# Setup of a graph and expert kernel: edges in 96 and 15 rows, weights loaded behind x and worked on behind table 1

## The chip, the cores and the metric

The kernel runs on one core of a Trainium2 chip. Its engines are TensorE (PE), VectorE (DVE), ScalarE (ACT), GpSimd (POOL) and SyncE (SP); sixteen DMA engines move data for all of them. The metric is the device time of one execution in microseconds, here the median of three runs.

## The reference

Four layers act on x, 6250 nodes by 256 features, each added to x. With LN the layer norm of a row:

```
h   = LN(x)
x  += GRU(segment_sum(h[src] + relvectors[edge_type], dst), h)      # 100000 edges, sorted by dst
x  += shared_mlp(LN(x)) + sum over the top 2 of 4 experts           # small experts
x  += segment_sum((LN(x) @ W.T + b)[src_i], tgt_i) / (deg + 1)
x  += top 2 of 8 experts, 256 -> 1024 -> 256 with gelu, on LN(x)
```

## The kernel before

The program is a sequence of blocks. In each, every engine has its own list of instructions, which it works through in order; semaphores order them among each other, and between two blocks all engines meet at a barrier. The first block is the setup. Behind it come the gather of layer 0 (POOL fetches rows of a table in DRAM, 128 edges an instruction, L748; PE adds them up by products with one-hot matrices, L817), the second gather, the experts, and the combination at the end.

The setup does three things.

The **edges**: SP waits until DVE has filled three tiles `edge_i` and then loads `dst`, `src` and `edge_type_16`. Each array has 100000 numbers, laid out as 896 to a partition: 111 full rows (L342) and a row of 544 (L344). The semaphore `edges_loaded` rises by 16 with each DMA. DVE turns them to floats (L485) and computes from them, in a long chain of small instructions (L489 to L587), which edges each tile of 128 nodes needs; PE turns them (L664), and DVE copies the turned ones (L514).

**x and table 1**: SP, behind the edges, issues x as one DMA (L347: 128 partitions, 48 rows of 1 KB each) and its tail of 106 rows (L349); they signal `x_loaded` and `x_tail_loaded`. `table1_groups` then runs over 12 groups of four tiles, two at a time in two sets of buffers, and a last group of one tile. For each group DVE takes the row statistics (`variance`, L193 and L197), ACT the square root (`ln_sqrt`, L214), DVE the reciprocal (L202), the two copies for later (L639, L640) and the normalised rows `h` (L207), ACT their half-precision copy `part` (L440), DVE the rest that the copy leaves (L648), and SP stores both as 512 KB of `table1` (L359), waiting for each store to land before the next.

The **weights**: ACT issues 30 loads (L403), 3.3 MB in all, many of them small or in 4-byte pieces, once the edges have landed. When the last of them has landed, ACT copies three of them to a reduced precision (L447 to L449), PE transposes the GRU's matrices and the second graph layer's into six banks (L698), ACT takes the high part of each (L457), DVE the low part (L614), and the last matrix only scaled (L619). DVE's `raw_copied` tells PE when a bank is free again.

Before the change the weights' part stands ahead of `table1_groups` in the lists of ACT and DVE, so the order on both is: weights, then table 1. The order of everything is written by hand; no scheduler has a part in it. `setup_chain` is a semaphore by which DVE waits for its own earlier results.

Of the kernel before, what the change touches and what calls it, by code (L numbers as in the profile page):

```python
# [16 lines left out]
F32 = mybir.dt.float32  # L17
# [3 lines left out]
ALU = mybir.AluOpType  # L21
# [4 lines left out]
P = 128  # L26
N = 6250
D = 256
C = D // P
# [9 lines left out]
EP, EJ = 112, 7  # L39
# [12 lines left out]
SCALE = 2048.0  # L52
# [13 lines left out]
TURN_CREDIT = 3  # L66
# [4 lines left out]
def program(nc, a, out):  # L71
# [6 lines left out]
    with ExitStack() as ctx:  # L78
        def sem(name):
            return ctx.enter_context(nc.semaphore(name))  # L80

        def sb(name, shape, dt, where=None):
            return (where or ctx).enter_context(nc.sbuf_tensor(name, shape, dt))

        bank = [ctx.enter_context(nc.psum_tensor(f"bank{i}", [P, 512], F32)) for i in range(8)]
# [46 lines left out]
        consts_ready = sem("consts_ready")  # L132
        loads_done = sem("loads_done")
        x_loaded = sem("x_loaded")
        x_tail_loaded = sem("x_tail_loaded")
# [83 lines left out]
        weights = {}  # L219

        Wr = sb("Wr", [P, C, E1], F32, graph)
        gcnT = sb("gcnT", [P, C, D], F32, graph)
# [19 lines left out]
        def split_wt(name, shape):  # L242
# [3 lines left out]
        wihT = split_wt("wihT", [P, C, 3 * D])  # L246
        whhT = split_wt("whhT", [P, C, 3 * D])
# [5 lines left out]
        sW3 = split_wt("sW3", [P, 1, D])  # L253
        eW2 = wt("eW2", [P, E0, 64])
        eW3 = split_wt("eW3", [P, 2, D])
        sel = sb("sel", [G_ROWS, E0 * 64], FR, layer0)
        bih = wt("bih", [P, 6])
        bhh = wt("bhh", [P, 6])
        brz = wt("brz", [P, 4])
        b_l1 = wt("b_l1", [P, 6])  # L260
        b_l2 = wt("b_l2", [P, 3])
        b_l3 = sb("b_l3", [G_ROWS, D], FR, layer0)
        gb = wt("gb", [P, E0])

        edge_i = [sb(f"edge_i{n}", [P, EJ * P], I32, setup) for n in range(3)]
# [22 lines left out]
        sW3_raw, eW3_raw, b_l3_raw, b_l3_low = (sb(name, [P, k, D], F32, setup)[:, :, :] for name, k in  # L288
                                                (("sW3_raw", 1), ("eW3_raw", 2), ("b_l3_raw", 1), ("b_l3_rest", 1)))
        b_l3_raw, b_l3_low = b_l3_raw[0:G_ROWS, 0, :], b_l3_low[0:G_ROWS, 0, :]  # L290
        is_high, is_low = (sb(f"is_{n}", [G_ROWS, 1], F32, setup) for n in ("high", "low"))
# [7 lines left out]
        def table1_groups(eng, stages):  # L299

            with eng.Fori(0, GROUPS // 2) as pair:
                both = [stages(pair * 2 + turn_, GW, turns[turn_]) for turn_ in range(2)]
                for steps in zip(*both):
                    for step in steps:
                        step()
            for step in stages(GROUPS, 1, turns[0]):
                step()
# [4 lines left out]
        edges_loaded = sem("edges_loaded")  # L312
# [8 lines left out]
        raw_turned = sem("raw_turned")  # L321
        raw_copied = sem("raw_copied")
        raw_high = sem("raw_high")
# [4 lines left out]
        s_hi = sem("s_hi")  # L328
        s_lo = sem("s_lo")
        s_out = sem("s_out")  # L330
        s_left = sem("s_left")
        WEIGHT_LOADS = 30

        with nc.Block() as block:
            @block.sync
            def _(sp):
                sp.wait_ge(edges_clear, 1)
                full = NE // (EJ * P)
                left = NE - full * EJ * P
                for n, name in enumerate(("dst", "src", "edge_type_16")):  # L340
                    e = a[name]
                    sp.dma_start(edge_i[n][0:full, :],  # L342
                                 e[0:full * EJ * P].rearrange("(p c) -> p c", p=full)).then_inc(edges_loaded, 16)
                    sp.dma_start(edge_i[n][full:full + 1, 0:left],  # L344
                                 e[full * EJ * P:NE].rearrange("(p c) -> p c", p=1)).then_inc(edges_loaded, 16)

                sp.dma_start(x_res[:, 0:(NT - 1) * D].rearrange("p (t d) -> p t d", d=D),  # L347
                             a["x"][0:(NT - 1) * P, :].rearrange("(t p) d -> p t d", p=P)).then_inc(x_loaded, 16)
                sp.dma_start(x_res[0:N - (NT - 1) * P, (NT - 1) * D:NT * D],  # L349
                             a["x"][(NT - 1) * P:N, :]).then_inc(x_tail_loaded, 16)  # L350

                sp.sem_inc(s_left, CREDIT + 1)
                sp.wait_ge(lohi_ready, 2)
                sp.dma_start(free_after[:, :], free_i[0:NT, :]).then_inc(free_stored, 16)

                def store(g, w, buffers):
                    part_ = buffers[5]
                    sp.wait_ge(s_lo, TURN_CREDIT + 2 * g + (2 if w > 1 else 1))
                    sp.dma_start(table1[ds(g * W, w * P), :].rearrange("(t p) d -> p t d", p=P),  # L359
                                 part_[:, 0:w, :]).then_inc(s_out, 16)  # L360
                    sp.wait_ge(s_out, 16 * g + 16)
                    sp.sem_inc(s_left, 1)

                table1_groups(sp, lambda g, w, buffers: [lambda: store(g, w, buffers)])
                sp.wait_ge(free_stored, 16)
# [31 lines left out]
            def _(act):  # L397
                n = 0
# [3 lines left out]
                    n += 1  # L402
                    act.dma_start(dst, src, allow_slow_non_contiguous=True).then_inc(loads_done, 16)  # L403

                act.wait_ge(edges_loaded, 6 * 16)
                load(wraw[0][:, :, :], a["L0_gnn_w_ih"].rearrange("(j p) i -> p j i", p=P))
                load(wraw[1][:, :, :], a["L0_gnn_w_hh"].rearrange("(j p) i -> p j i", p=P))
                load(wraw[2][:, :, :], a["L1_gnn_W"].rearrange("(j p) i -> p j i", p=P))
# [34 lines left out]
                    return [lambda: ln_sqrt(act, s_var, s_std, g, w, mean_var_, stdev_, True), high]  # L443


                act.wait_ge(loads_done, 16 * n)
                nc.scalar.activation(sW3[0][:, :, :], sW3_raw, ACT.Copy).then_inc(raw_high, 1)  # L447
                nc.scalar.activation(eW3[0][:, :, :], eW3_raw, ACT.Copy).then_inc(raw_high, 1)
                nc.scalar.activation(b_l3[:, :], b_l3_raw, ACT.Copy).then_inc(raw_high, 1)  # L449
                turned = 0  # L450
                for dst, blocks in ((wihT, 6), (whhT, 6)):
                    for c in range(C):
                        for j0 in range(0, blocks, 4):
                            k = min(4, blocks - j0)
# [1 line left out]
                            act.wait_ge(raw_turned, turned)  # L456
                            nc.scalar.activation(dst[0][:, c, j0 * P:(j0 + k) * P], bank[(turned - 1) % 6][:, 0:k * P],  # L457
                                                 ACT.Copy).then_inc(raw_high, 1)
                act.wait_ge(consts_ready, 4)
                act.sem_inc(s_lo, TURN_CREDIT)  # L460
                act.sem_inc(s_hi, TURN_CREDIT)
                table1_groups(act, stages)
                act.wait_ge(loads_done, 16 * n)

            @block.vector
            def _(dve):
                chain = Chain(dve, "setup_chain", 96)
# [12 lines left out]
                nc.vector.tensor_copy(ts_idx[:, :, :], iw[4][:, :].rearrange("p (t j) -> p t j", j=E1))  # L480
                nc.vector.tensor_scalar(kmb[:, :], iw[3][:, :], BIG, None, ALU.subtract)
                chain.link(nc.vector.tensor_scalar(kidx[:, :], iw[3][:, :], 1.0, None, ALU.add))
                dve.wait_ge(edges_loaded, 6 * 16)
                for n in range(3):
                    nc.vector.tensor_copy(edge_f[n][0:EP, :], edge_i[n][0:EP, :]).then_inc(edges_float, 1)  # L485
                dve.wait_ge(edges_float, 3)
# [20 lines left out]
                for n in range(3):  # L507
                    dst = (dstT, srcT, typeT)[n]
                    c0 = 0 if n == 1 else U
                    view = dst[:, c0:c0 + CHUNKS].rearrange("p (k j) -> p j k", j=EJ)  # L510
                    for half in range(2):
                        dve.wait_ge(edges_turned, 2 * n + half + 1)
                        j0, k = (0, 4) if half == 0 else (4, 3)
# [76 lines left out]
                def columns(first):  # L590
# [3 lines left out]
                                        ALU.add)  # L594
                nc.vector.tensor_reduce(is_high[:, :], ident[0:G_ROWS, 0:G_AGAIN], AX, ALU.add)
                chain.link(nc.vector.tensor_reduce(is_low[:, :], ident[0:G_ROWS, G_AGAIN:G_ROWS], AX, ALU.add))
                dve.wait_ge(loads_done, 16 * weights["loads"])
                dve.wait_ge(raw_high, 3)
                nc.vector.tensor_tensor(sW3[1][:, :, :], sW3_raw, sW3[0][:, :, :].bitcast(F32), ALU.subtract)
                nc.vector.tensor_tensor(eW3[1][:, :, :], eW3_raw, eW3[0][:, :, :].bitcast(F32), ALU.subtract)  # L600
                chain.link(nc.vector.tensor_tensor(b_l3_low, b_l3_raw, b_l3[:, :].bitcast(F32), ALU.subtract))
                chain.link(nc.vector.tensor_scalar(b_l3_low, b_l3_low, is_low[:, 0:1], None, ALU.mult))
                chain.link(nc.vector.scalar_tensor_tensor(b_l3[:, :], b_l3[:, :].bitcast(F32), is_high[:, 0:1], b_l3_low,
                                                          ALU.mult, ALU.add))

                turned = 0
                for dst, blocks in ((wihT, 6), (whhT, 6)):
                    for c in range(C):
                        for j0 in range(0, blocks, 4):
                            k = min(4, blocks - j0)  # L610
                            turned += 1
                            dve.wait_ge(raw_high, 3 + turned)
                            o = slice(j0 * P, (j0 + k) * P)
                            nc.vector.tensor_tensor(dst[1][:, c, o], bank[(turned - 1) % 6][:, 0:k * P],  # L614
                                                    dst[0][:, c, o].bitcast(F32), ALU.subtract).then_inc(raw_copied, 1)
                for c in range(C):
                    turned += 1
                    dve.wait_ge(raw_turned, turned)
                    nc.vector.tensor_scalar(gcnT[:, c, :], bank[(turned - 1) % 6][:, 0:D], 1.0 / SCALE, None,  # L619
                                            ALU.mult).then_inc(raw_copied, 1)  # L620
                chain.link(nc.vector.tensor_tensor(brz[:, :], bih[:, 0:4], bhh[:, 0:4], ALU.add))
                chain.end()


                variance_chain, rstd_chain = Chain(dve, "variance_chain", 1), Chain(dve, "rstd_chain", 1)
                dve.wait_ge(x_loaded, 16)
                dve.wait_ge(x_tail_loaded, 16)
# [23 lines left out]
                    return [variance, normalise, first_rest]  # L651

                table1_groups(dve, stages)

            @block.tensor
            def _(pe):
# [1300 lines left out]
```

## Time and profile before

| | us |
|---|---|
| median of three runs (3719.65 to 3723.12) | 3721.45 |
| the profiled execution | 3720.04 |
| its span, first to last instruction | 3718.5 |

| engine | busy us | share of the span |
|---|---|---|
| PE | 2435.0 | 65% |
| DVE | 1525.3 | 41% |
| ACT | 779.4 | 21% |
| POOL | 1833.6 | 49% |

The span is one execution taken by the profiler; the runs are others, without it. Busy shares are averages over blocks with different limits and say little about the setup, in which DVE is busy for two thirds of the time and POOL hardly at all. A timeline row gives start, duration, engine, line, operation, the tile written and the tile read; in brackets stands how long the engine had been idle and what ended that. SPq and ACTq are the sequencers of SP and ACT issuing a DMA: the duration is that of the issue, not of the transfer. In the rows on DMA, q1 is SP's queue and q10 is ACT's.

### The profile page before, as it was taken

How to read it: one execution, taken by the hardware profiler on the slowest of the kernel's cores; microseconds unless marked ns; L12 is line 12 of the kernel's file. 1: busy time of each engine (PE TensorE's matmuls, PEld its weight loads, DVE VectorE, ACT ScalarE, POOL GpSimd, SP SyncE). 2: the span in 40 equal slices, each digit the busy share in tenths (PEclk: the TensorE clock that was granted, in tenths of full speed). 3: DMA queues.
4: the chain of work that ended last, by engine and by line, in shares of the span. 5: the costliest groups of instructions: out<-in, count | busy, mean ns of one | idle time of the engine just before them, and what ended most of it. 6: DMA issues, size and time to landing. Idle time of an engine off the chain costs nothing. (4 is left out here: it accounts for less than half of the span.)

```text
span 3718.5 us, 54160 instructions
## 1 busy us (share of the span) xinstructions
PE 2435.0 (65%) x13318; PEld 1841.3 (50%) x13319; DVE 1525.3 (41%) x3970; ACT 779.4 (21%) x1414; POOL 1833.6 (49%) x2044
## 2 busy tenths in 40 slices
PE   1278887877877674355666655444432499999992
PEld 1255555555544452134444433332221399999992
DVE  6444444444444432034454433232320344545545
ACT  1222232222221121020000000000000145545441
POOL 0363434444565666616666666666666344444441
PEclk7578887888878776566766666556655699999996
DMA  5221222222233222223333333322332222211215
GB/s 135 90 84 57 64 59 66 65 66 65 79 90 86 86 82 86 85 54 88 87 95 88 88 87 89 89 86 83 88 87 85 66 66 85 65 46 64 64 44 219
DMA packets 157829, 303.02 MB, mean 81 GB/s; under 512 B 47366, under 2 KB 91817, under 8 KB 157753
## 3 DMA queue, kind: packets, MB, share of 16 engines
q0 software_dynamic: 85984, 234.74, 21.9%
q1 hardware_dynamic: 40876, 36.11, 3.2%
q10 hardware_dynamic: 30892, 31.40, 2.5%
q14 instruction: 58, 0.47, 0.0%
q8 instruction: 19, 0.31, 0.0%
HBM read 261.73 MB, written 40.39 MB: 81 GB/s over the span
## 5 line engine op out<-in xcount | busy, mean ns | idle before, releaser
L748 POOL DMA_INDIRECT rows<-table,srcT x1568 | 1532.8, 978 | 1172.8 <-DMA rows<-table,srcT 477.6
L817 PE MATMUL bank<-rows,onehot 128*128 x3904 | 763.4, 352 | 818.8 <-POOLq L736 617.2
L817 PEld LDWEIGHTS bank<-rows,onehot 128*128 x3904 | 448.2, 115 | 1118.6 <-issue 967.8
L778 DVE SCALAR_TENSOR_TENSOR onehot<-iota_row,tbase,dstT 128x512 f16 x488 | 366.7, 752 | 783.2 <-issue 506.7
L1779 PE MATMUL bank<-xe_high,W_high 128*128 128x256 f32 x864 | 252.8, 293 | 30.2 <-DVE xe_low L1857 29.9
L1829 ACT ACTIVATE hid<-bank,b 128x256 f32<-128x256 f32 x432 | 181.2, 471 | 346.5 <-PE bank L1781 345.4
L1780 PE MATMUL bank<-xe_low,W_high 128*128 128x256 f32 x864 | 250.6, 290 | 0.0
L1781 PE MATMUL bank<-xe_high,W_low 128*128 128x256 f32 x864 | 250.3, 290 | 0.0
L1779 PE MATMUL bank<-W_high,hid_high 128*128 128x256 f32 x864 | 248.3, 287 | 0.0
L1865 DVE TENSOR_TENSOR hid_low<-hid,hid_high 128x512 fp32r<-128x512 f32 x216 | 149.6, 692 | 235.3 <-ACT hid_high L1833 235.3
L1781 PE MATMUL bank<-W_high,hid_low 128*128 128x256 f32 x864 | 243.9, 282 | 0.0
L1780 PE MATMUL bank<-W_low,hid_high 128*128 128x256 f32 x864 | 243.8, 282 | 0.0
L1468 ACT ACTIVATE sumsT<-bank 128x512 f32<-128x512 f32 (+2 forms) x28 | 13.7, 541 | 872.6 <-PE bank L1423 854.5
L1779 PEld LDWEIGHTS bank<-xe_high,W_high 128*128 128x128 f32 x864 | 171.9, 199 | 32.6 <-issue 32.6
L1733 POOL DMA_INDIRECT xs<-normal,rows_of x110 | 141.2, 1283 | 65.8 <-POOL rows_of L1729 46.3
L1780 PEld LDWEIGHTS bank<-xe_low,W_high 128*128 128x128 f32 x864 | 171.8, 199 | 0.0
L1781 PEld LDWEIGHTS bank<-xe_high,W_low 128*128 128x128 f32 x864 | 171.5, 198 | 0.0
L1780 PEld LDWEIGHTS bank<-W_low,hid_high 128*128 128x128 f32 x864 | 164.5, 190 | 0.0
L1779 PEld LDWEIGHTS bank<-W_high,hid_high 128*128 128x128 f32 x864 | 164.4, 190 | 0.0
L1781 PEld LDWEIGHTS bank<-W_high,hid_low 128*128 128x128 f32 x864 | 164.3, 190 | 0.0
L1742 POOL DMA_INDIRECT results<-ys,to_old x112 | 110.4, 986 | 70.2 <-POOL to_new L1723 53.1
L1833 ACT ACTIVATE hid_high<-hid 128x512 fp32r<-128x512 f32 x216 | 136.5, 632 | 6.9
(338 smaller groups left out, 3591.2 us busy)
## 6 DMA issues: line engine op xcount, KB each, us to landing
rows<-table,srcT POOLq DMA_INDIRECT x1568
W<-in_L_ffn_W_dram SPq DMA_DIRECT2D x14, 1024.0 KB
y<-results ACTq DMA_DIRECT2D x12, 1024.0 KB, 9.9
x_res<-in_x_dram SPq DMA_DIRECT2D x1, 6144.0 KB, 43.0
out_dram<-x_res SPq DMA_DIRECT2D x12, 512.0 KB
table<-part ACTq DMA_DIRECT2D x11, 512.0 KB
normal<-xn ACTq DMA_DIRECT2D x11, 512.0 KB
table<-part SPq DMA_DIRECT2D x6, 512.0 KB, 2.9
```

The costliest lines, as they stand in the source:

```text
L748: nc.gpsimd.indirect_dma_start(out=rows[:, k % (M * U), 0:ROW], out_offset=None, in_=q.table, in_offset=bass.IndirectOffsetOnAxis(srcT[:, ...
L778: last = nc.vector.scalar_tensor_tensor(onehot[:, ds(slot, U), :], iota_row[:, :].unsqueeze(1).to_broadcast([P, U, P]), base, dstT[:, ds(k ...
L817: last = nc.tensor.matmul(acc[:, 0:cols], hot, ring_rows[:, ds(row0 + (s * q.pitch + at), cols)], start=False, stop=False, skip_group_chec ...
L1468: last = nc.scalar.activation(sumsT[:, c, 0:w * P], bank[c][:, 0:w * P], ACT.Copy)
L1733: nc.gpsimd.indirect_dma_start(out=xs[:, s, :], out_offset=None, in_=normal, in_offset=bass.IndirectOffsetOnAxis(rows_of[:, s:s + 1], axis ...
L1742: nc.gpsimd.indirect_dma_start(out=results, out_offset=bass.IndirectOffsetOnAxis(to_old[:, s:s + 1], axis=0), in_=ys[:, s, :], in_offset=N ...
L1779: nc.tensor.matmul(acc, w_high, m_high, start=start, stop=False)
L1780: nc.tensor.matmul(acc, w_high, m_low, start=False, stop=False)
L1781: return nc.tensor.matmul(acc, w_low, m_high, start=False, stop=stop)
L1829: nc.scalar.activation(hid[:, hc, :], bank[1 + pair][:, o:o + TT], ACT.Gelu, bias=b1[b][:, hc:hc + 1]).then_inc(X["gelu_done"], 1)
L1833: nc.scalar.activation(hid_high[:, both, :], hid[:, both, :], ACT.Copy).then_inc(X["hid_high"], 1)
L1865: nc.vector.tensor_tensor(hid_low[:, both, :], hid[:, both, :], hid_high[:, both, :].bitcast(F32), ALU.subtract).then_inc(X["hid_ready"], 1)
```

## The change

Three edits, all in the setup block.

Each edge array is loaded by three DMAs: 96 rows, 15 rows and the rest of 544. `edges_loaded` therefore counts nine. ACT's 30 loads wait for x and its tail, no longer for the edges. And in the lists of ACT and DVE `table1_groups` stands ahead of the weights' part. PE's and POOL's lists are as they were; PE still waits for all loads and the edges before it turns the weights.

```diff
-        WEIGHT_LOADS = 30
+        EDGE_LOADS = 9
...
                 full = NE // (EJ * P)
                 left = NE - full * EJ * P
+                even = full // 16 * 16
                 for n, name in enumerate(("dst", "src", "edge_type_16")):
                     e = a[name]
-                    sp.dma_start(edge_i[n][0:full, :],
-                                 e[0:full * EJ * P].rearrange("(p c) -> p c", p=full)).then_inc(edges_loaded, 16)
+                    for p0, p1 in ((0, even), (even, full)):
+                        sp.dma_start(edge_i[n][p0:p1, :],
+                                     e[p0 * EJ * P:p1 * EJ * P].rearrange("(p c) -> p c", p=p1 - p0)).then_inc(edges_loaded, 16)
                     sp.dma_start(edge_i[n][full:full + 1, 0:left],
                                  e[full * EJ * P:NE].rearrange("(p c) -> p c", p=1)).then_inc(edges_loaded, 16)
...
-                act.wait_ge(edges_loaded, 6 * 16)
+                act.wait_ge(x_loaded, 16)
+                act.wait_ge(x_tail_loaded, 16)
                 load(wraw[0][:, :, :], a["L0_gnn_w_ih"].rearrange("(j p) i -> p j i", p=P))
...
+                act.wait_ge(consts_ready, 4)
+                act.sem_inc(s_lo, TURN_CREDIT)
+                act.sem_inc(s_hi, TURN_CREDIT)
+                table1_groups(act, stages)
                 act.wait_ge(loads_done, 16 * n)
                 nc.scalar.activation(sW3[0][:, :, :], sW3_raw, ACT.Copy).then_inc(raw_high, 1)
...
-                act.wait_ge(consts_ready, 4)
-                act.sem_inc(s_lo, TURN_CREDIT)
-                act.sem_inc(s_hi, TURN_CREDIT)
-                table1_groups(act, stages)
-                act.wait_ge(loads_done, 16 * n)
...
-                dve.wait_ge(edges_loaded, 6 * 16)
+                dve.wait_ge(edges_loaded, EDGE_LOADS * 16)
...
                 chain.link(nc.vector.tensor_reduce(is_low[:, :], ident[0:G_ROWS, G_AGAIN:G_ROWS], AX, ALU.add))
+                variance_chain, rstd_chain = Chain(dve, "variance_chain", 1), Chain(dve, "rstd_chain", 1)
+                dve.wait_ge(x_loaded, 16)
+                dve.wait_ge(x_tail_loaded, 16)
+
+                def stages(g, w, buffers):
...
+                table1_groups(dve, stages)
+
                 dve.wait_ge(loads_done, 16 * weights["loads"])
                 dve.wait_ge(raw_high, 3)
                 nc.vector.tensor_tensor(sW3[1][:, :, :], sW3_raw, sW3[0][:, :, :].bitcast(F32), ALU.subtract)
...
                 chain.end()
-
-
-                variance_chain, rstd_chain = Chain(dve, "variance_chain", 1), Chain(dve, "rstd_chain", 1)
-                dve.wait_ge(x_loaded, 16)
-                dve.wait_ge(x_tail_loaded, 16)
-
-                def stages(g, w, buffers):
...
-                table1_groups(dve, stages)
```

The function `stages` is moved as it is.

On ACT, around the last of its loads, the list of before has the weights (`sW_high`, `eW_high`, `b_l`, `wihT_high`, `whhT_high`) between the last load and the square root:

```order
L403 DMA br<-in_L_ffn_br_dram 128x8
L447 ACT_TABLE_LOAD
L447 ACTIVATE sW_high<-sW_raw 128x256 [waits loads_done]
L448 ACTIVATE eW_high<-eW_raw 128x512
L449 ACTIVATE b_l<-b_l_raw 14x256
L457 ACTIVATE wihT_high<-bank 128x512 [waits raw_turned]
```

In the list now, the same place:

```order
L405 DMA br<-in_L_ffn_br_dram 128x8
L301 UNCONDITIONAL_BRANCH [waits consts_ready]
L301 ISA
L214 ACT_TABLE_LOAD
L214 ACTIVATE stdev<-mean_var,eps_scaled 128x4 [waits s_var]
L213 REGISTER_ALU
L214 ACTIVATE stdev_b<-mean_var_b,eps_scaled 128x4 [waits s_var]
L443 ACTIVATE part<-h 128x2x256 [waits s_left,s_h] x2
```

One table load is gone, and the loop of table 1 comes straight behind the loads. The first load carries the new wait:

```order
L398 UNCONDITIONAL_BRANCH [waits barrier_Pool_Activation_PE_DVE_SP_release]
L405 DMA rows<-in_L_gnn_w_ih_dram 128x6x256 [waits x_tail_loaded,x_loaded]
L405 DMA rows<-in_L_gnn_w_hh_dram 128x6x256
L405 DMA rows<-in_L_gnn_W_dram 128x2x256
L405 DMA relvec<-in_L_gnn_relvectors_dram 16x256
```

Everything of ACT stands behind that wait. On DVE, where table 1 ends and the weights' low parts begin, the list now reads:

```order
L207 TENSOR_SCALAR h<-x_res,mean_var,rstd 128x256 [waits s_hi]
L622 TENSOR_TENSOR part<-h,part 128x256 [waits s_hi,s_h]
L631 TENSOR_TENSOR sW_low<-sW_raw,sW_high 128x256 [waits raw_high,loads_done]
L632 TENSOR_TENSOR eW_low<-eW_raw,eW_high 128x512
L633 TENSOR_TENSOR b_l_rest<-b_l_raw,b_l 14x256
L634 TENSOR_SCALAR b_l_rest<-b_l_rest,is_low 14x256 [waits setup_chain]
```

Before, `part` of the last group was DVE's last instruction of the block, and `sW_low` stood directly behind the edges' chain (`is_low`, L596).

## Rows read from the trace of the kernel before

**Rows 1.** The page, costliest groups: line engine op, count, busy, mean ns, idle.

```profile
L748 POOL DMA_INDIRECT rows<-table,srcT x1568 | 1532.8, 978 | 1172.8 <-DMA rows<-table,srcT 477.6
```

**Rows 2.** Timeline of SP: start us, duration us, engine, line, op, tiles.

```profile
4.24 0.38 SPq L342 DMA_DIRECT2D edge_i<-in_dst_dram  x1
...
5.95 3.96 SPq L344 DMA_DIRECT2D edge_i<-in_edge_type_dram  x1
9.96 0.74 SPq L347 DMA_DIRECT2D x_res<-in_x_dram  x1
10.74 34.47 SPq L349 DMA_DIRECT2D x_res<-in_x_dram  x1
...
134.77 0.35 SPq L359 DMA_DIRECT2D table<-part  x1
```

**Rows 3.** Stretches: from:to, length, busy of five engines, PE clock, DMA share, GB/s.

```profile
5.80:10.00 4.20, 0.00 (x0) 0.00 (x0) 0.00 (x0) 0.00 (x0) 0.00 (x0) 1.00 0.18 67
12.00:27.70 15.70, 0.00 (x0) 0.00 (x0) 0.00 (x0) 0.00 (x0) 0.00 (x0) 1.00 1.10 240
28.00:32.00 4.00, 2.86 (x13) 2.89 (x14) 3.56 (x6) 0.00 (x0) 0.00 (x0) 1.00 1.10 349
53.10:56.20 3.10, 0.49 (x4) 0.40 (x4) 2.17 (x20) 0.00 (x0) 0.00 (x0) 0.50 0.34 59
```

**Rows 4.** DMA queues, 53.1 to 56.2 us: kind, packets, MB, share of 16 engines.

```profile
q1 hardware_dynamic: 82, 0.08, 7.5%
```

**Rows 5.** DMA queues, 32 to 62 us: ACT's queue.

```profile
q10 hardware_dynamic: 8092, 3.34, 43.1%
```

**Rows 6.** Timeline of ACT, its loads and the ends of the setup.

```profile
28.29 0.43 ACTq L403 DMA_DIRECT2D rows<-in_L_gnn_w_ih_dram  x1
...
29.34 2.96 ACTq L403 DMA_DIRECT2D rows<-in_L_gnn_W_dram  x1
...
34.31 3.89 ACTq L403 DMA_DIRECT2D bhh<-in_L_gnn_b_hh_dram  x1
...
56.46 1.27 ACTq L403 DMA_DIRECT2D b_l_raw<-in_L_ffn_eb_dram  x3
...
58.76 0.45 ACTq L403 DMA_DIRECT2D br<-in_L_ffn_br_dram  x1
59.24 1.28 ACT L447 ACT_TABLE_LOAD   x1 [59.08 <-issue]
62.11 0.42 ACT L447 ACTIVATE sW_high<-sW_raw 128x256 fp32r<-128x256 f32 x1 [1.58 <-DMA br<-in_L_ffn_br_dram]
...
62.95 0.40 ACT L449 ACTIVATE b_l<-b_l_raw 14x256 fp32r<-14x256 f32 x1
...
72.83 0.30 ACT L214 ACTIVATE stdev<-mean_var,eps_scaled 128x4 f32<-128x4 f32 x1 [3.47 <-DVE mean_var L197]
...
131.54 0.42 ACT L440 ACTIVATE part<-h 128x256 f16<-128x256 f32 x1 [1.01 <-SPq L362]
```

**Rows 7.** Timeline of DVE, 28 to 138 us.

```profile
28.37 1.70 DVE L485 CAST edge_f<-edge_i 112x896 f32<-112x896 int32 x3 [23.08 <-DMA edge_i<-in_edge_type_dram]
...
58.89 0.14 DVE L596 TENSOR_REDUCE is_low<-ident 14x1 f32<-14x5 f32 x1
63.48 0.43 DVE L599 TENSOR_TENSOR sW_low<-sW_raw,sW_high 128x256 fp32r<-128x256 f32 x1 [4.45 <-ACT b_l L449]
...
70.13 0.15 DVE L621 TENSOR_TENSOR brz<-bih,bhh 128x4 f32<-128x4 f32 x1
70.86 1.41 DVE L193 BATCH_NORM_STATS2 stats<-x_res 128x6 f32 x4 [0.57 <-DVEq L167]
...
74.57 0.14 DVE L202 RECIPROCAL rstd<-stdev 128x4 f32<-128x4 f32 x1
...
132.06 0.43 DVE L648 TENSOR_TENSOR part<-h,part 128x256 f16<-128x256 f32 x1 [0.76 <-ACT part L440]
137.05 0.06 DVE L1322 MEMSET gate_rows<- 128x4 f32 x1 [4.56 <-PEq L334]
```

More of the change, by code:

```diff
@@ L596, in _, with variance, normalise, first_rest @@
                 chain.link(nc.vector.tensor_reduce(is_low[:, :], ident[0:G_ROWS, G_AGAIN:G_ROWS], AX, ALU.add))
+                variance_chain, rstd_chain = Chain(dve, "variance_chain", 1), Chain(dve, "rstd_chain", 1)
+                dve.wait_ge(x_loaded, 16)
+                dve.wait_ge(x_tail_loaded, 16)
+                def stages(g, w, buffers):
+                    stats_, mean_var_, stdev_, rstd_, h4_, part_ = buffers
+                    def variance():
+                        variance_chain.begin(g)
+                        ln_variance(dve, variance_chain, s_var, w, g * GW, stats_, mean_var_)
+                    def normalise():
+                        rstd_chain.begin(g)
+                        ln_rstd_(dve, rstd_chain, s_std, g, w, stdev_, rstd_)
+                        nc.vector.tensor_copy(ln_mean[:, ds(g * GW, w)], mean_var_[:, 0:w, 0])
+                        nc.vector.tensor_scalar(ln_rstd[:, ds(g * GW, w)], rstd_[:, 0:w], 1.0 / SCALE, None, ALU.mult)
+                        dve.wait_ge(s_hi, TURN_CREDIT + 2 * g - 2)
+                        ln_apply(g * GW, w, h4_, mean_var_, rstd_).then_inc(s_h, 1)
+                    def first_rest():
+                        dve.wait_ge(s_h, g + 1)
+                        for half, lo, k in halves(w):
+                            dve.wait_ge(s_hi, TURN_CREDIT + 2 * g + half + 1)
+                            nc.vector.tensor_tensor(part_[:, lo:lo + k, D:2 * D], h4_[:, lo:lo + k, :],
+                                                    part_[:, lo:lo + k, 0:D], ALU.subtract).then_inc(s_lo, 1)
+                    return [variance, normalise, first_rest]
+                table1_groups(dve, stages)
                 dve.wait_ge(loads_done, 16 * weights["loads"])
@@ L622, in _ @@
                 chain.end()
-                variance_chain, rstd_chain = Chain(dve, "variance_chain", 1), Chain(dve, "rstd_chain", 1)
-                dve.wait_ge(x_loaded, 16)
-                dve.wait_ge(x_tail_loaded, 16)
-                def stages(g, w, buffers):
-                    stats_, mean_var_, stdev_, rstd_, h4_, part_ = buffers
-                    def variance():
-                        variance_chain.begin(g)
-                        ln_variance(dve, variance_chain, s_var, w, g * GW, stats_, mean_var_)
-                    def normalise():
-                        rstd_chain.begin(g)
-                        ln_rstd_(dve, rstd_chain, s_std, g, w, stdev_, rstd_)
-                        nc.vector.tensor_copy(ln_mean[:, ds(g * GW, w)], mean_var_[:, 0:w, 0])
-                        nc.vector.tensor_scalar(ln_rstd[:, ds(g * GW, w)], rstd_[:, 0:w], 1.0 / SCALE, None, ALU.mult)
-                        dve.wait_ge(s_hi, TURN_CREDIT + 2 * g - 2)
-                        ln_apply(g * GW, w, h4_, mean_var_, rstd_).then_inc(s_h, 1)
-                    def first_rest():
-                        dve.wait_ge(s_h, g + 1)
-                        for half, lo, k in halves(w):
-                            dve.wait_ge(s_hi, TURN_CREDIT + 2 * g + half + 1)
-                            nc.vector.tensor_tensor(part_[:, lo:lo + k, D:2 * D], h4_[:, lo:lo + k, :],
-                                                    part_[:, lo:lo + k, 0:D], ALU.subtract).then_inc(s_lo, 1)
-                    return [variance, normalise, first_rest]
-                table1_groups(dve, stages)
             @block.tensor
```

## The prediction

> **What bounds the kernel now.** I read the page first. Its costliest groups belong to the gather of the first layer and to the second feed-forward stage [rows 1]; the change touches neither. It lies inside the setup, and all that comes later starts behind a barrier, so the question is when the setup ends. The timelines of DVE, ACT and SP give that: the last instruction of the setup's own work on DVE ends at 132.5, SP stores the last group of table 1 at 134.77, and DVE's first instruction of the next stage starts at 137.05 [rows 2, 6, 7]. The 1568 gather instructions of 0.98 us, which stand one behind another on POOL in two of the later stages [rows 1], start when the barrier opens, whenever that is. I take it that an earlier barrier moves everything behind it by the same amount.
>
> Backwards from 137.05: table 1 is a pipeline of DVE and ACT, in which DVE hardly idles; from its first reciprocal at 74.57 to its last subtraction at 132.49 it takes 57.9 us [rows 7]. Before it stand, on DVE and ACT, the splitting and turning of the weights (62.11 to 70.28), and before those ACT's thirty DMA issues, from 28.29 to 59.21, and the landing of the last at 62.1 [rows 6, 7]. So now the chain is: edges landed (28.3), thirty issues (30.9), landing (2.9), weights (8.2), first statistics, table (57.9), last store. DVE's own long chain on the edges, 28.37 to 59.03, ends while this goes on and costs nothing [rows 7].
>
> Why do 1.2 MB of edges, issued from 4.24, land only at 28.3? The stretch table shows it: from 5.8 to 10 the DMA engines are busy for a share of 0.18, which is three engines of sixteen (0.19), at 67 GB/s; and until 27.7 they are all busy but move 240 GB/s, while right after the edges, with x alone on the queue, it is 349 [rows 3]. The 111 rows lie on three engines (111 is 3 times 37), and those three then also carry their share of x. x's tail of 106 rows (2 times 53) runs last: from 53.1 to 56.2 SP's queue holds 7.5% of sixteen engines, 1.2 engines' time [rows 4]. x is complete at about 56.3. While three engines lag, ACT's loads, which need all sixteen, lag with them.
>
> The rule for this stands in the Trainium skill, "DMA: Bandwidth & Descriptors", section "Why a DMA increments its semaphore by 16 and not by 1": a copy takes the largest number of engines up to 16 that divides its slowest dimension. The trace agrees with it for 111 and for 106 rows; no row shows 96 or 15, for which it says 16 and 15. If it failed for them, that would be rival C below.
>
> **Part 1, edges as 96 and 15 rows.** Three more issues on SP. Five issues took from 4.24 to 5.95, 0.34 each [rows 2], so nine end at 7.3, where x's issue begins; before, it was 9.96, because the sixth was held 3.96 us. First data came 1.6 us behind the first issue; x's came 2 us behind its own [rows 2, 3]. On all engines 1.2 MB at 349 GB/s are 3.4 us [rows 3]: edges landed at about 9.6 rather than 28.3, x's data from 9.5. x is 6.29 MB: 18.0 us at 349, so 27.5; its tail on two engines another 3.2 [rows 4]: 30.7. Bounds: if x alone runs at the 240 GB/s of the stretch with the edges, it is 26.2 and lands at 38.9 [rows 3]. I take 349, the rate of x alone once the edges are in.
>
> The same page, section "Bandwidth", gives 425 GB/s for a single core's 16 MB load. By that x would take 14.8 us and the result would be 3 us lower; the row with x alone shows 349, and I stay with it.
>
> **Part 2, ACT's loads wait for x and its tail.** They begin at 30.9 instead of 28.29, so they start 2.6 us later, but their duration matters more, since all the ACT work of table 1 is behind them in the queue. Thirty issues took 30.9 us while x was on the engines. The last seven, issued from 56.46 to 59.21 when x had landed, took 2.75: 0.39 each [rows 6]. Thirty at that price are 11.8. The engines' own time for ACT's 8092 packets is 43.1% of 30 us, 12.9 us [rows 5], so it can't be below 13. The long ones before (third 2.96, sixth 3.89) were held by queues that were not drained [rows 6]; with no x beside them the first 1.8 MB still need 5 us at 349, and that holds the fifth to eighth issue for about as long. I take 13 + 5.5 = 18.5; bounds 13 and 30.9. ACT is free at 49.4.
>
> **Part 3, table 1 first.** ACT loads its table (1.28) and takes the first square root (0.30) [rows 6]: DVE's first reciprocal, 74.57 before, starts at 51.1. DVE must be there too: edges at 9.6 plus its chain of 30.7 is 40.3, plus 0.6 and the first two statistics (3.7, from 70.86 to 74.57) 44.6 [rows 7]. That is 6 us of cover; if ACT is quicker than I think, DVE ends it at 44.6. The pipeline itself is unchanged, 57.9 us: it ends at 109.0 instead of 132.5, 23.5 earlier. The loads that are still landing behind ACT's last issue are for nobody before the table's end.
>
> **Part 4, the weights behind it.** Three copies on ACT (62.11 to 63.35, 1.24), during which DVE ends its last group; then DVE's splitting, 63.48 to 70.28, 6.8 us [rows 6, 7]. PE has long put the first six banks in place by then, which spares ACT short waits, but DVE had none here before, so it gains nothing. ACT's last table copy ends at 131.96 - 23.5 = 108.5; plus 1.24, plus 0.13, plus 6.8 is 116.7. The last store, which set the end before (134.77, landed before 137.05), now lands at 113.5 beneath this. With 0.4 for the barrier the next stage starts at 117.1. This part costs: behind the table's end there were 4.56 us, now there are 8.1, so 3.5 more.
>
> **Sum.** 23.5 - 3.5 = 20.0 us earlier. The profiled execution took 3720.04 us (span 3718.5), 1.4 below the median of the runs, 3721.45. 3720.04 - 20.0 + 1.4 is 3701.5. In general the gain is 74.57 less the start of the first reciprocal, less 3.5; it is zero where that starts at 71.1.
>
> **Rivals.**
> A. One of the two prices is at its upper end. If ACT's thirty issues take 30.9 again (held by something other than x's packets), the first reciprocal is at 63.5: gain 7.6, 3713.9. If x runs at 240, it is at 59.3: gain 11.8, 3709.7. For it: no row shows these loads without x. Against it: 0.39 an issue once x had landed.
> B. Both at once: 38.9 + 30.9 + 1.7 is 71.5, gain -0.4: 3721.9, no change. The weights' work has been put at the end, and the head start pays for just that. Against it speaks that both prices were measured beside the crowded three engines.
> C. Slower: ACT now waits for something that comes late. If 96 or 15 rows do not spread and x with its tail is complete only at 56.3 as now [rows 4], ACT's queue issues from 56.4; with the 30.9 us that it took in that neighbourhood, the first reciprocal is at 88.9: 14.3 later, plus 3.5, is 17.8: 3739. It decides from 71.1 on. For it: the wait on the tail is new, and behind it ACT holds all square roots; against it: the share of 0.18 says that three engines are the trouble, and 96 is six times 16.
> D. The gain is larger: ACT needs only 13 us for its issues. Then DVE's 44.6 against ACT's 45.5 are nearly even, the first reciprocal is at 45.5, gain 25.6: 3695.8.
>
> **Numbers.** Forecast (first reciprocal between 47 and 57): 0.58. A: 0.20. B: 0.08. C: 0.06. D: 0.08. A change of 0.2% is 7.4 us, about what a measurement here can tell. Forecast, D and most of A are faster by more than that: 0.84; B and the edge of A are within it: 0.10; C is slower: 0.06. The range goes from D to the upper end of A: 3695 to 3714.
>
> **What would show it.** In the profile of the changed kernel: DVE's first edge cast near 10 instead of 28.37; 350 GB/s from 10 to 28; ACT's first issue near 31 and its last ending near 49; no wait of DVE between the edges' chain and the first statistics, but a wait of some 5 us before its first reciprocal, named ACT; that reciprocal near 51; last subtraction of table 1 near 109; DVE's weight work right behind, unbroken, 6.8 us; next stage at 117. If ACT's issues end near 62, it is A; if its first is near 56, C. If the setup ends near 117 and the time is still above 3710, then what is behind the barrier did not just move, and my first assumption is wrong.

## The result, and the profile after

| | before | after |
|---|---|---|
| median, us | 3721.45 (9 runs, 3703.3 to 3732.0) | 3692.58 (9 runs, 3686.4 to 3702.1) |
| profiled execution | 3720.04 | 3699.73 |
| its span | 3718.5 | 3698.1 |
| the setup ends (DVE's first instruction behind it) | 137.05 | 116.12 |

The ratio is 0.9925, with a 95% interval of 0.9906 to 0.9944. Of 3721.45 that is a gain of 27.9 us, between 20.8 and 35 (the two medians themselves lie 28.9 apart). The forecast was 20.0 and 3701.5; the measured 3692.58 lies 2.4 us under the lower end of the range. The profiled executions differ by 20.3 us, their setups by 20.9. So the change does in the setup what the working said, and the question is what the other 7 us are.

The timeline of SP after, against [rows 2]; columns are start, duration, engine, line, operation:

```profile
4.24 0.93 SPq L344 DMA_DIRECT2D edge_i<-in_dst_dram  x2
...
7.43 0.25 SPq L346 DMA_DIRECT2D edge_i<-in_edge_type_dram  x1
7.73 0.43 SPq L349 DMA_DIRECT2D x_res<-in_x_dram  x1
8.20 14.96 SPq L351 DMA_DIRECT2D x_res<-in_x_dram  x1
...
110.93 0.35 SPq L361 DMA_DIRECT2D table<-part  x1
```

Nine issues fill 4.24 to 7.73, 0.39 us each, none is held, and x is issued at 7.73 instead of 9.96. x's tail is held for 15 us, not 34.5. The stretches after, against [rows 3]:

```profile
5.80:7.00 1.20, 0.00 (x0) 0.00 (x0) 0.00 (x0) 0.00 (x0) 0.00 (x0) 1.00 0.84 286
12.00:27.00 15.00, 7.91 (x44) 7.54 (x44) 14.59 (x21) 0.00 (x0) 0.00 (x0) 0.94 1.10 349
28.00:31.40 3.40, 0.43 (x4) 0.19 (x4) 2.59 (x19) 0.00 (x0) 0.00 (x0) 0.50 0.33 107
30.00:31.00 1.00, 0.00 (x0) 0.00 (x0) 0.90 (x8) 0.00 (x0) 0.00 (x0) 0.50 0.11 39
31.40:48.30 16.90, 2.11 (x8) 1.05 (x8) 11.54 (x73) 0.00 (x0) 0.00 (x0) 0.50 0.77 200
```

The edges now use most of the engines (0.84 instead of 0.18), so 96 and 15 rows do spread, and from 12 to 27 x moves at 349 GB/s instead of 240. In the stretch from 28 the rest of x runs out and the tail is left: the mean share is 0.33, from 30 to 31 it is 0.11, less than two engines' time, and at 31.4 all is done. The timeline of ACT, against [rows 6]:

```profile
31.43 0.43 ACTq L405 DMA_DIRECT2D rows<-in_L_gnn_w_ih_dram  x1
...
32.48 0.57 ACTq L405 DMA_DIRECT2D rows<-in_L_gnn_W_dram  x1
...
34.46 1.16 ACTq L405 DMA_DIRECT2D bhh<-in_L_gnn_b_hh_dram  x1
...
47.81 0.45 ACTq L405 DMA_DIRECT2D br<-in_L_ffn_br_dram  x1
48.59 1.28 ACT L214 ACT_TABLE_LOAD   x1 [48.43 <-issue]
49.89 0.30 ACT L214 ACTIVATE stdev<-mean_var,eps_scaled 128x4 f32<-128x4 f32 x1
...
107.19 0.42 ACT L443 ACTIVATE part<-h 128x256 f16<-128x256 f32 x1 [1.02 <-SPq L364]
107.51 0.40 ACT L454 ACTIVATE sW_high<-sW_raw 128x256 fp32r<-128x256 f32 x1
...
108.33 0.40 ACT L456 ACTIVATE b_l<-b_l_raw 14x256 fp32r<-14x256 f32 x1
...
113.00 0.87 ACT L464 ACTIVATE whhT_high<-bank 128x512 fp32r<-128x512 f32 x2 [2.05 <-PE bank L699]
```

The third and the sixth issue, 2.96 and 3.89 us before, are 0.57 and 1.16. Thirty issues take 16.8 us instead of 30.9. The table load and the square root follow at once. PE has six banks and fills the seventh turn only when DVE has freed one, so at the end ACT has to wait 2.05 us for it; DVE does not wait with it. The timeline of DVE, against [rows 7]:

```profile
12.14 1.70 DVE L487 CAST edge_f<-edge_i 112x896 f32<-112x896 int32 x3 [6.85 <-DMA edge_i<-in_edge_type_dram]
...
42.66 0.14 DVE L598 TENSOR_REDUCE is_low<-ident 14x1 f32<-14x5 f32 x1
43.17 1.41 DVE L193 BATCH_NORM_STATS2 stats<-x_res 128x6 f32 x4 [0.38 <-DVE is_low L598]
...
50.22 0.18 DVE L202 RECIPROCAL rstd<-stdev 128x4 f32<-128x4 f32 x1 [3.24 <-ACT stdev L214]
...
107.71 0.43 DVE L622 TENSOR_TENSOR part<-h,part 128x256 f16<-128x256 f32 x1 [0.78 <-ACT part L443]
108.83 0.42 DVE L631 TENSOR_TENSOR sW_low<-sW_raw,sW_high 128x256 fp32r<-128x256 f32 x1 [0.70 <-ACT b_l L456]
...
115.49 0.15 DVE L653 TENSOR_TENSOR brz<-bih,bhh 128x4 f32<-128x4 f32 x1
116.12 0.06 DVE L1323 MEMSET gate_rows<- 128x4 f32 x1 [0.48 <-PEq L334]
```

DVE starts on the edges 16.2 us sooner, ends its chain at 42.8, takes the first statistics and then waits 3.24 us for ACT's square root. From the first reciprocal to the last subtraction are 57.9 us, as before. The weights' work, 108.83 to 115.64, is unbroken, and 0.48 us later the next stage begins.

### The profile page after: what moved, and what is told of

It reads as the page before. It is cut to its first block and busy times, and to the rows that moved or that the text cites. A ratio compares the mean times of both kernels' runs of the same rounds, so it can differ in the third digit from the quotient of the medians.

```text
span 3698.1 us, 54162 instructions
## 1 busy us (share of the span) xinstructions
PE 2417.0 (65%) x13318; PEld 1821.9 (49%) x13319; DVE 1525.1 (41%) x3970; ACT 776.4 (21%) x1413; POOL 1836.0 (50%) x2044
## 5 line engine op out<-in xcount | busy, mean ns | idle before, releaser
L1743 POOL DMA_INDIRECT results<-ys,to_old x112 | 110.4, 986 | 70.2 <-POOL to_new L1724 53.1
```

Of the source, the lines that this page charges most:

```text
L1743: nc.gpsimd.indirect_dma_start(out=results, out_offset=bass.IndirectOffsetOnAxis(to_old[:, s:s + 1], axis=0), in_=ys[:, s, :], in_offset=N ...
```

## The experiments

Theory 1 says that the setup's end moves all that follows by as much, and that the rest of the measured difference is the scatter of executions. Theory 2 says that some 8 us are gained behind the setup as well. What follows takes the change apart and then tests the two. In the expectations, parts 1 to 4 are those of the prediction: the edges' rows, ACT's wait for x and its tail, table 1 first, the weights behind it. A gain in us is (1 - ratio) times the median of before in the same comparison; an interval in brackets is its 95% interval.

**The changed kernel again** (no edit).

> The changed kernel once more, unchanged. Its profile ended the setup 20.9 us sooner than before (116.1 against 137.05), its profiled execution was 20.3 us shorter, but the medians lie 28.9 apart. Theory 1 (everything behind the setup just moves; the rest is scatter between executions, which spans 29 us over nine runs of before): the setup ends at 116.1 again, and the ratio comes nearer to 0.9944 (20.9 us), between 0.992 and 0.996; the stretches behind the setup differ between the two profiles of this kernel by some us. Theory 2 (some 8 us are gained behind the setup as well, in every execution): the ratio is 0.9922 again, and the two profiles agree behind the setup within 1 us.

The setup ended at 116.05. Ratio 0.9935 (0.9921 to 0.9949), a gain of 23.6 us (18.5 to 28.6). Nearer to 21 than to 28, but the interval holds both. The level of all runs was another: before had a median of 3623.67 us here, 98 us less than in the first comparison. Of this more below. It also spoils the second half of the test, whether the two profiles agree behind the setup; profiles of one level are compared below the table.

**Part 1 alone**: the edges' edit in the kernel before, nothing else.

```diff
-                    sp.dma_start(edge_i[n][0:full, :],
...
+                    for p0, p1 in ((0, even), (even, full)):
+                        sp.dma_start(edge_i[n][p0:p1, :],
...
-                act.wait_ge(edges_loaded, 6 * 16)
+                act.wait_ge(edges_loaded, 9 * 16)
```

> Part 1 alone: edges in 96 and 15 rows; ACT's loads still wait for the edges alone, and the weights stand ahead of table 1. If the three crowded engines were the cause of nearly all: edges at 12.1, ACT's first issue at 12.3, the thirty issues take 20 to 25 us beside x on even engines, the last load landed at 36 to 41 or so; DVE's chain on the edges ends at 42.8 and is then what the weights wait for; first reciprocal at about 55, no weights behind the table: setup ends near 118, gain 19 us. Rival (the new order does it): ACT's issues beside x take 31 us again and more, landed at 46 to 50, first reciprocal at 60, setup ends at 123, gain 14 or less.

Ratio 0.9956 (0.9942 to 0.9970): 15.9 us (10.9 to 21.0). Its timeline of ACT, the longest wait of DVE (in all, times, longest), and the setup's end on DVE:

```profile
11.41 0.43 ACTq L405 DMA_DIRECT2D rows<-in_L_gnn_w_ih_dram  x1
...
13.03 3.18 ACTq L405 DMA_DIRECT2D rows<-in_L_gnn_W_dram  x1
...
18.12 3.97 ACTq L405 DMA_DIRECT2D bhh<-in_L_gnn_b_hh_dram  x1
...
44.07 0.45 ACTq L405 DMA_DIRECT2D br<-in_L_ffn_br_dram  x1
44.55 1.28 ACT L449 ACT_TABLE_LOAD   x1 [44.39 <-issue]
47.41 0.42 ACT L449 ACTIVATE sW_high<-sW_raw 128x256 fp32r<-128x256 f32 x1 [1.57 <-DMA br<-in_L_ffn_br_dram]
```

```profile
DVE sW_low L601 <- ACT b_l L451: 6.7, 1, 6.7
```

```profile
122.31 0.06 DVE L1324 MEMSET gate_rows<- 128x4 f32 x1 [4.54 <-PEq L334]
```

The rival was right here. Beside x the issues take as long as before even with x evenly spread, 33.1 us, and the third and sixth are held as they were (3.18, 3.97). So what holds ACT's queue is x, not the three crowded engines. It isn't SP's own issue of the tail either, which ended at 29.15 here (8.21 plus 20.94): ACT's issues between 33 and 41 still took 1.0 to 2.4 us each, and went down to 0.46 at 41.27, when x had landed (7.74 plus 32.9). The last load lands at 47.4, DVE waits 6.7 us for it, and the setup ends 14.7 us sooner.

**Parts 2 to 4 without part 1**: the changed kernel, its wait on x included, with the edges in 111 rows.

```diff
-        EDGE_LOADS = 9
+        EDGE_LOADS = 6
...
-                    for p0, p1 in ((0, even), (even, full)):
-                        sp.dma_start(edge_i[n][p0:p1, :],
...
+                    sp.dma_start(edge_i[n][0:full, :],
```

> Parts 2 to 4 alone: edges in 111 rows as before, ACT's loads behind x and its tail, table 1 ahead of the weights. By the working of rival C with the measured 16.8 us for thirty issues: x and tail at 56.3, issues 56.4 to 73.3, table load, first reciprocal at 75.3 (before: 74.57), setup ends at 141.2, loss 4 us: 3725. If ACT's issues take 31 us whatever is beside them: first reciprocal 89, loss 18 us.

Ratio 0.9977 (0.9966 to 0.9988): a gain of 8.3 us (4.3 to 12.3), where I expected a loss. The first and last of ACT's loads, two stretches, and DVE's first reciprocal and the setup's end:

```profile
47.28 0.43 ACTq L403 DMA_DIRECT2D rows<-in_L_gnn_w_ih_dram  x1
...
63.53 0.45 ACTq L403 DMA_DIRECT2D br<-in_L_ffn_br_dram  x1
```

```profile
28.00:37.00 9.00, 7.74 (x41) 7.77 (x42) 8.28 (x13) 0.00 (x0) 0.00 (x0) 1.00 0.89 283
40.00:47.00 7.00, 0.48 (x4) 0.24 (x4) 6.08 (x23) 0.00 (x0) 0.00 (x0) 0.50 0.18 63
```

```profile
65.94 0.18 DVE L202 RECIPROCAL rstd<-stdev 128x4 f32<-128x4 f32 x1 [2.63 <-ACT stdev L214]
...
131.83 0.06 DVE L1321 MEMSET gate_rows<- 128x4 f32 x1 [0.48 <-PEq L334]
```

x and its tail were complete at 47.3, not at 56.3. With no weights beside them the three slow engines get through 9 us sooner; from 40 to 47 the mean share is 0.18, three engines' time, and nothing else is on them. ACT's thirty issues, from 47.28 to 63.98, took 16.7 us. I had priced rival C with a time that was itself made by the loads which the change moves away. The setup ends 5.2 us sooner. So the wait and the new order together pay without part 1, too.

**Parts 1 and 2, weights ahead of table 1**: the kernel of part 1 alone, with ACT's wait on x and its tail.

```diff
-                act.wait_ge(edges_loaded, 9 * 16)
+                act.wait_ge(x_loaded, 16)
+                act.wait_ge(x_tail_loaded, 16)
```

> Parts 1 and 2 without the new order: edges in 96 and 15 rows, ACT's loads behind x and tail, weights ahead of table 1. Issues 31.4 to 48.3, landed at 51.2, weights 51.2 to 59.4, first reciprocal 12.5 behind the landing at 63.7, setup ends at 126.2: gain 10.9 us, half of the full change's. If the order of the lists were worth nothing, the gain would be that of the full change, 20.9.

Ratio 0.9969 (0.9958 to 0.9980): 11.2 us (7.2 to 15.2). DVE's first weight instruction, first reciprocal and the setup's end:

```profile
52.46 0.42 DVE L602 TENSOR_TENSOR sW_low<-sW_raw,sW_high 128x256 fp32r<-128x256 f32 x1 [9.92 <-ACT b_l L452]
...
63.56 0.14 DVE L202 RECIPROCAL rstd<-stdev 128x4 f32<-128x4 f32 x1
...
125.98 0.06 DVE L1325 MEMSET gate_rows<- 128x4 f32 x1 [4.54 <-PEq L334]
```

As worked out to 0.3 us. Waiting for x costs 3.7 us against part 1 alone while the weights are first, because their landing is on the chain. With table 1 first only the end of the issues is on it, and the new list order is worth 9.9 us on top of this kernel (125.98 against 116.05). The setup's 21.0 us are thus 14.7 for the edges, -3.7 for the wait and 9.9 for the order.

**Two delays**: the changed kernel with 22 and with 11 fills at the end of DVE's setup work.

```diff
+                for _ in range(22):
+                    chain.link(nc.vector.memset(edge_i[1][:, :], 0))
                 chain.end()
```

> The changed kernel with 22 fills of a setup tile (0.81 us each, 0.95 with their wait) put at the end of DVE's setup work, so that the setup ends at 137.0, where it ended before the change. It separates where the setup ends from how it gets there. Theory 1 (only the end counts): the same as before, ratio 0.9985 to 1.0015. Theory 2 (the changed setup speeds up what follows by some 8 us): ratio 0.998 or lower, about 8 us under before, with the stretches behind the setup shorter by that.

> The same with 11 fills: the setup ends at 126.6. Theory 1: gain 10.5 us, ratio 0.997. Theory 2 with a cause in the alignment (what follows depends on when it starts): a gain away from the line through the other kernels by over 5 us, 5 or less or 16 or more.

The end of the edit on DVE, in the kernel with 22:

```profile
116.64 0.15 DVE L653 TENSOR_TENSOR brz<-bih,bhh 128x4 f32<-128x4 f32 x1
117.04 0.81 DVE L655 MEMSET edge_i<- 128x896 int32 x1 [0.25 <-DVE brz L653]
...
140.55 0.06 DVE L1325 MEMSET gate_rows<- 128x4 f32 x1 [0.47 <-PEq L334]
```

A fill with its wait is 1.06 us, so the setup ended at 140.55, 3.5 us behind before, not level with it. Ratio 1.0007 (0.9993 to 1.0020): 2.6 us slower (from 2.6 faster to 7.4 slower). With the changed layout of the setup but without its earlier end nothing is gained. Theory 2 would have had it 4.5 us faster, outside the interval. The kernel with 11 ended its setup at 127.40, 9.7 us sooner than before, and gained 4.5 us (0 to 8.5). That missed the 10.5 of theory 1 and, taken alone, is the value that theory 2 with a cause in the alignment asked for (5 or less); it was measured again below.

**The loads behind the edges**: the changed kernel with ACT's old wait.

```diff
-                act.wait_ge(x_loaded, 16)
-                act.wait_ge(x_tail_loaded, 16)
+                act.wait_ge(edges_loaded, EDGE_LOADS * 16)
```

> The changed kernel with ACT's loads behind the edges again instead of behind x (parts 1, 3 and 4). Beside x the thirty issues took 33 us in the kernel with part 1 alone (11.4 to 44.5), behind it 16.8. So ACT is free at 45, first square root at 46.2, DVE ready at 46.3: first reciprocal at 47 instead of 50.2, setup ends at 113, gain 24. If keeping the weights away from x is what pays, it is slower than the changed kernel: first reciprocal past 52.

Ratio 0.9935 (0.9916 to 0.9954): 24.2 us (17.1 to 31.3). DVE's first reciprocal and the setup's end:

```profile
46.56 0.18 DVE L202 RECIPROCAL rstd<-stdev 128x4 f32<-128x4 f32 x1
...
112.50 0.09 DVE L1322 MEMSET gate_rows<- 128x4 f32 x2 [0.48 <-PEq L334]
```

ACT's issues took 33.1 us but began 20 us sooner, so ACT was free at 44.6 rather than 48.3 and the setup ended 3.6 us before the changed kernel's. With the edges in 96 and 15 rows the wait on x is the one part of the change that costs, in this order (3.6 us of setup) as in the other (3.7); with 111 rows it was not tried apart. In measured time this kernel and the changed one can't be told apart.

**SP issues the loads, and each edge array is waited for by itself**: the thirty loads move from ACT's list to SP's, behind x's tail, and `edges_loaded` becomes three semaphores.

```diff
-                    act.dma_start(dst, src, allow_slow_non_contiguous=True).then_inc(loads_done, 16)
+                    sp.dma_start(dst, src, allow_slow_non_contiguous=True).then_inc(loads_done, 16)
...
+                def to_float(n):
+                    dve.wait_ge(edges_loaded[n], 3 * 16)
```

> The changed kernel with the thirty loads issued by SP behind x's tail, and DVE waiting for each edge array by itself (dst landed near 7.5 us in the changed kernel's trace, all three near 12). If the chain is now ACT's queue up to the first square root, and then DVE's chain on the edges: DVE's first cast at 7.6, its edge chain ends at 38.3, statistics, first reciprocal at 42.6, setup ends at 108.5: gain 28.5 us on before, 7.6 on the changed kernel. If SP's issues keep its stores of table 1 back, the stores wait and the first groups slip: setup ends past 112.

Ratio 0.9938 (0.9921 to 0.9955): 23.0 us (16.7 to 29.4). The first and last of SP's loads, and DVE:

```profile
23.98 2.57 SPq L359 DMA_DIRECT2D rows<-in_L_gnn_w_ih_dram  x1
...
46.14 0.43 SPq L359 DMA_DIRECT2D br<-in_L_ffn_br_dram  x1
```

```profile
8.06 0.63 DVE L486 CAST edge_f<-edge_i 112x896 f32<-112x896 int32 x1 [2.77 <-DMA edge_i<-in_dst_dram]
...
38.85 0.14 DVE L601 TENSOR_REDUCE is_low<-ident 14x1 f32<-14x5 f32 x1
...
43.08 0.14 DVE L202 RECIPROCAL rstd<-stdev 128x4 f32<-128x4 f32 x1
...
109.65 0.06 DVE L1326 MEMSET gate_rows<- 128x4 f32 x1 [0.48 <-PEq L334]
```

DVE casts `dst` at 8.1, and no longer waits for ACT before its first reciprocal at 43.1. The first reciprocal is 7.1 us sooner than in the changed kernel: 3.8 because the edges' chain ends at 39.0 instead of 42.8, the rest because the wait of 3.24 for ACT is gone. The two edits were not run apart. The setup ends at 109.65, 6.4 us before the changed kernel's.

**Four more**, measured side by side on one chip: the kernel before against itself, the changed kernel a third time, the one with 11 fills and the one with SP's loads again (edits as above).

> The kernel before against itself. Both theories: ratio 1, the setup ends at 137.05. What it tells is how far a comparison of this kind strays with nothing changed: if the 8 us that the first comparison showed beyond the setup's 20.9 were scatter of executions, a ratio off 1 by 0.001 (4 us) with an interval of about +-0.0015 is to be expected here too; if the intervals of such comparisons are honest to 2 us, theory 1 is in trouble.

> The changed kernel a third time. Theory 1: gain 21 us, ratio 0.9935 to 0.995 depending on the level of the runs, so that the mean over the three comparisons falls towards 0.9940. Theory 2: 28 us, 0.9925.

> The kernel with 11 fills again, whose setup ends at 127.4, 9.65 us before that of before. Its first comparison gave a gain of 4.5 us (0 to 8.5), the farthest from the line of all on the low side. Theory 1: 9.7 us this time within 4. If the time of what follows depends on when it starts, it is 4.5 us again, while the changed kernel beside it gains 21 or more.

> The version with SP's loads and an edge wait for each array again, beside the changed kernel on the same chip. Its setup ended at 109.7, 6.4 us before that of the changed kernel: by theory 1 a gain of 27.4 us on before, ratio 0.9925, and 6.4 us less than the changed kernel of this call.

All thirteen comparisons, by the setup's end:

| kernel | setup ends at | sooner than 137.05 by | gain measured, us (95%) |
|---|---|---|---|
| changed, first comparison | 116.12 | 20.9 | 27.9 (20.8 to 35.0) |
| changed, again | 116.05 | 21.0 | 23.6 (18.5 to 28.6) |
| changed, third | 116.35 | 20.7 | 20.3 (14.5 to 26.1) |
| part 1 alone | 122.31 | 14.7 | 15.9 (10.9 to 21.0) |
| parts 1 and 2 | 125.98 | 11.1 | 11.2 (7.2 to 15.2) |
| parts 2 to 4 | 131.83 | 5.2 | 8.3 (4.3 to 12.3) |
| 22 fills | 140.55 | -3.5 | -2.6 (-7.4 to 2.6) |
| 11 fills | 127.40 | 9.7 | 4.5 (0 to 8.5) |
| 11 fills, again | 128.14 | 8.9 | 12.7 (8.3 to 17.0) |
| loads behind the edges | 112.50 | 24.6 | 24.2 (17.1 to 31.3) |
| SP's loads | 109.65 | 27.4 | 23.0 (16.7 to 29.4) |
| SP's loads, again | 109.52 | 27.5 | 28.3 (22.8 to 33.7) |
| before against itself | 137.95 | -0.9 | 0.4 (-4.0 to 4.7) |

The gain follows the setup's end one for one, within the scatter. The differences of the last two columns lie between -5.2 and +7.0 and are 0.8 on average. The first comparison is the farthest out, and the kernel with 11 fills went from 5.2 below the line to 3.8 above it with nothing changed. That speaks against a cause in when the later stages start, and the third comparison of the changed kernel, 20.3, against a steady gain of 28. The profiles say it without any median. From the setup's end to the end of the span, the first pair took 3581.4 us (before) and 3582.0 (changed); at the lower level the kernel before took 3485.5, the changed one 3486.8 and 3487.1. That stretch scatters by itself, over 7 us among the profiles of the upper level and 13 among those of the lower, but it is nowhere shorter by 8 us for the changed kernel. Theory 1 stands. Weighted by their intervals, the three comparisons of the changed kernel give 23.4 us, within 3.4; its 20.9 are inside. The version with SP's loads ended its setup 6.4 and 6.8 us before the changed kernel's; where both were measured side by side, its median was 3594.8 against 3603.8. It is faster than the kernel before beyond doubt, and faster than the changed one by the median and by the setup's end, though the intervals of the two (14.5 to 26.1 and 22.8 to 33.7) still overlap.

## Why the prediction was right and where it was wrong

The mechanism was right, the time came out below the range.

- *The chain.* Right. Every stop of it was in the profile: edges at 12.1 (said 9.6), ACT's first issue 31.4 (30.9), its last ending 48.3 (49.4), first reciprocal 50.2 (51.1), table 1 done at 108.1 (109.0), next stage 116.1 (117.1).
- *Part 1.* The rate of x was right, 349 GB/s. The edges took longer: they keep the engines at a share of 0.84 while SP issues, and x, issued at 7.73, already ran beside them: from 7 to 12 SP's queue moved 1.26 MB, when at most 0.86 MB of edges were left. They landed at 12.1. The working had them alone on the engines. That ate near half of the 6 us of cover that DVE's chain was to have (its wait for ACT is 3.24), and cost nothing.
- *Part 2.* 16.8 us for thirty issues against 18.5; the 5.5 us added to the engines' 13 were 1.7 too many. The reason given, x's packets, was right: part 1 alone showed 33.1 beside an evenly spread x. Rival A, in which something else held them or x ran at 240, is out.
- *Part 4.* From table 1's end to the next stage are 8.0 us (108.14 to 116.12) where 4.56 stood before: 3.4 more, against 3.5. The 0.4 for the barrier had no row behind it; it was 0.48.
- *The sum.* 20.9 in place of 20.0, and the span 20.4 shorter.
- *The step that failed* is the last one: the term of 1.4 us that turns a profiled execution into a median, and the range, which gave that term no width. The sum took the profiled execution of before, 1.4 under its median, and put the same 1.4 on the changed kernel. There the profiled execution, 3699.73, lay 7.1 above the median of its nine runs: 3720.04 - 20.3 - 7.1 is the measured 3692.6. So of the 8.9 us under the forecast, 0.3 is the profiled executions' difference (20.3 for 20.0) and 8.6 is this term. As far as the runs show it is scatter: in the two repeats the profiled execution lay 3.2 and 1.1 above the median, and the gains by the medians were 22.4 and 19.9. The three runs shown (3719.65 to 3723.12) made the scatter look small; nine runs of the same kernel spread over 3703.3 to 3732.0, and a comparison can lie up to 7 us from the setup's own gain. The lower end, 3695, held D's mechanism and no scatter. With 7 us on either side the range would have been 3688 to 3721. What makes single executions differ stays open.
- *The bound for no change.* I took 0.2%, 7.4 us, for what can be told from no change. The intervals here are 4 to 7 us to either side, so that was about right, and should have widened the range as well.
- *Rival C's price* was wrong by 23 us (first reciprocal at 65.94, said 88.9) though its condition, three engines, held in the kernel with parts 2 to 4. Of these, 9 are x: its 56.3 was not a fact about 111 rows but about 111 rows with the weights beside them, and it was 47.3. The other 14 are ACT's issues, 16.7 us and not 30.9. It was a gain. So the chance of a slower kernel stood on numbers that the change itself removed.
- *The gathers.* The prediction has the 1568 gathers stand one behind another on POOL. Its own row shows 1172.8 us of idle time before them [rows 1], so POOL alone does not set these stages; the last section shows what else does. The assumption drawn from it, that all behind the barrier just moves, held to 2 us in the profiles of the changed kernel beside those of before.

## What to carry to other kernels

Look up on how many engines a transfer runs before anything else in a load stage: here a share of 0.18 in a stretch that should have been full meant three engines of sixteen, and splitting 111 rows into 96 and 15 was worth 14.7 us alone. A queue of small DMAs on a compute engine costs that engine its issue time, here 16.8 us for thirty and 33.1 beside a large transfer; if its own work stands behind them, give the issues to an engine that is idle. Where a stage is serial, its end predicts the gain better than few medians do: forecast the stage from the trace and the range from the spread of many runs.

## What the runs showed that I had not expected

The same program ran at two levels, near 3720 us in two series of runs and near 3624 in two others, a difference far larger than anything here. One chip showed both. It lies in one stage, the gather of layer 0: from the setup's end to the first instruction of the next gather it took 1520.4 us (116.1 to 1636.5) in the first profile of the changed kernel and 1424.7 (116.0 to 1540.7) in the second, while the following gather took 1298.2 and 1299.0. The other profiles fall in with these: 1515.9 to 1520.9 at the upper level, 1417.5 to 1429.9 at the lower. For each of the two follow the stretch from 400 to 1000 us, the last columns being PE's granted clock (a mean; single stretches above show 1.00 or 0.50), DMA share and GB/s, and then POOL's wait for PE in that stage (total us, times, longest). The first profile, 1520.4 us:

```profile
400.00:1000.00 600.00, 480.58 (x2142) 322.12 (x2141) 267.19 (x706) 156.07 (x255) 274.54 (x280) 0.83 0.23 67
```

```profile
POOL rows L749 <- PE bank L818: 252.7, 37, 20.2
```

The second, 1424.7 us:

```profile
400.00:1000.00 600.00, 499.63 (x2426) 327.06 (x2425) 301.33 (x812) 177.11 (x287) 319.54 (x328) 0.91 0.26 78
```

```profile
POOL rows L749 <- PE bank L818: 147.7, 32, 15.1
```

PE's mean granted clock is 0.83 of full speed in the one and 0.91 in the other; POOL waits 105 us less for PE to free its buffers. So this stage is in part bound by PE. That the clock makes the difference is likely, but not shown: a PE that is fed less evenly may also be the reason for its lower clock, and one run of the first kernel with SP's loads took 3697.93 us, within the upper level, at a mean clock of 0.761 over the whole execution, where the others of that level had 0.738 to 0.748. What made the level differ was not tried. It also means that "everything behind the setup just moves" holds for the mean: that stage alone varied by 12 us among the profiles of the lower level (1417.5 in the kernel with part 1 alone, 1429.9 in the second one with SP's loads).
